# Input loads reordered, read weights cut to a quarter, all measured differences on GpSimd

## The chip, the cores and the metric

One core of one Trainium2 chip. The metric is the device time of one launch in microseconds. Engines in profile rows: PE is TensorE (PEld its weight loads), DVE is VectorE, ACT is ScalarE, POOL is GpSimd, SP is SyncE; a q behind a name is the engine's queue of instructions that issue DMAs.

## The reference

x is 1024 tokens (2 batches of 512) of 1024 channels, read as 256 heads by C = 4. Cut to what matters:

```
r = layernorm(x)                                   # the front: per token
y_o = sum_c r[h, c] * W[h, o, c]                   # "read": o = 0..2 gives q, k, v inputs
q, k, v = norm(y_o) @ qkv_w[o]; q, k = rope(q, k, pos)
a = causal softmax attention, 16 heads of 16       # then a "write" that mixes a into r
mlp: read (2 outputs), ctx as weights, silu * up, and a second write
x = x + r
W1, W2, W3 = base + mean(|w - base|) * sign(w - base)
x = x + (silu(ln(x) @ W1.T) * (ln(x) @ W3.T)) @ W2.T     # 3584 inner channels
```

The two scalars mean(|w - base|) of w1 and w3 need every element of both before the first product with a blended weight; w2's is measured later.

## The kernel before

The program has two phases. Phase one (to about 410 us) computes the attention part for 8 tiles of 128 tokens and, beside it, measures w1 and w3. Phase two is the large feed-forward product, bound by TensorE.

Phase one is cut into nodes (stage, tile, part), each on one engine. `phase_one_order` puts them in one order by the table RANK (a node is taken when all it depends on has been taken, lowest rank first), and each engine runs its own nodes in that order, waiting on semaphores. The tables WORK, LOADED and DIFFERENCE hold the planner's costs and load times; they change nothing but the assignment of banks.

The stages: `front` (per tile: layer norm statistics on DVE, power on POOL, scaling on ACT L1790, turning on PE L1406, copy L1795, read products with a block-diagonal weight `diag` on PE L1444, statistics L2129, power L2545, scaling L1803, turning, copy, qkv products L1459, rotation on DVE L2164 to L2172, turning, copy). `diag` (DVE L2336) multiplies the read weights w_in by an eye of 32 columns; it uses only rows 32c to 32c + 31 of channel c of w_in. `fill` (scores into the PSUM area quad, twice for each group of 4 heads: S for the row maxima, T turned), `use` (DVE maxima L2182 for S, ACT exponentials L1830 for T), `turnmax` (PE L1489, DVE L2191), `weigh` and `out` (PE L1479, ACT), `row`, `back` (first write and second read), `mlp`, `finish` (second write), `norm`, `turn`, `early` (the first feed-forward products).

`measure` t (0 to 55, one weight tile of 128 x 1024 each): SP loads w and base into one of three slots (L1280, L1281), the difference is taken on DVE in one instruction (L2388) or on POOL in four pieces (L2551), ACT sums the absolute values (L1878), and the slot is free. MEASURER gives 38 of the 56 to DVE (t mod 3 is 0 or 1) and 18 to POOL. Slots 1 and 2 share memory with the mlp's ctx up to t = 29, and measures from 30 on wait for the first batch's attention. `coef` needs all 56 sums, `prep` and `upper` blend the first weight tiles; ACT's first copy into xnT_hi waits for all 56 as well.

The start: SP issues ident, cmask, pos, inv and gb, then x0, x1, w_in0, wqkv, x2, x3, w_in1, x4, x5, then both write weights, and the measure loads. PE, DVE and ACT wait for the five constants (ld_const at 80). DVE then makes unit, maskb, eyer, the angles and, after ACT's two sines, the rotation tables and eye, all ahead of its first node. ACT makes the sines and waits for the tables (rope_ok) ahead of its first node. `lull` puts filler products (bf16, `unit` times `unit`, 512 columns, L1415) ahead of some PE nodes, as many as LULLS says.

## Time and profile before

| | us |
|---|---|
| median of 3 runs | 1199.28 (1198.12 to 1204.73) |
| the profiled execution's own time | 1198.74 |
| its span | 1197.0 |
| PE busy | 1162.5 (97%) |
| DVE busy | 944.9 (79%) |
| ACT busy | 714.4 (60%) |
| POOL busy | 367.9 (31%) |

The span is that of one execution as the profiler saw it. Busy time is the union of an engine's instructions; PE's ends are modelled, so a busy PE isn't one at its peak. In the stretches PEclk is the granted share of the full TensorE clock of 2.4 GHz.

### The profile page before, as it was taken

Reading aid. Unit: us, or ns where it says so; the run is one execution under the profiler, and the core shown is the slowest. Engines: PE = TensorE matmul, PEld = TensorE weight load, DVE = VectorE, ACT = ScalarE, POOL = GpSimd, SP = SyncE. Lnnn points to the kernel's source line nnn. Section 1 sums busy time; section 2 is a strip of 40 time slices with the busy share of each in tenths; the row PEclk is TensorE's granted clock in tenths of the full one; section 3 lists DMA queues with packets and bytes.
Section 4 is the critical chain, followed back from the end, with each engine's and each line's share of the span. In section 5 each row is a group of like instructions: output and inputs, shape, how many; then the busy total and the mean of one; then the engine's idle time right before and its main releaser. Section 6 shows DMA issues by size and latency. Waiting matters only on the chain.

```text
span 1197.0 us, 17179 instructions
## 1 busy us (share of the span) xinstructions
PE 1162.5 (97%) x6218; PEld 909.0 (76%) x6218; DVE 944.9 (79%) x1279; ACT 714.4 (60%) x1017; POOL 367.9 (31%) x441
## 2 busy tenths in 40 slices
PE   6998899999999999999999999999999999999998
PEld 4765565657777787888888888888888888888887
DVE  6878899788989688777877778777885687888764
ACT  3887776867778566665666556565663433333342
POOL 2333534444543424443344424353330000000000
PEclk8999999999999999999999999999999999999999
DMA  8377796645431566687667867678756968752332
GB/s 354 135 272 284 272 342 217 233 180 189 159 104 55 194 187 223 220 271 244 198 220 231 281 189 250 193 247 265 220 184 233 358 230 288 254 201 91 104 132 97
DMA packets 99064, 257.37 MB, mean 215 GB/s; under 512 B 9362, under 2 KB 23972, under 8 KB 98468
## 3 DMA queue, kind: packets, MB, share of 16 engines
q1 hardware_dynamic: 94948, 241.59, 56.0%
q0 software_dynamic: 4032, 14.68, 6.9%
q8 instruction: 50, 0.82, 0.3%
q14 instruction: 34, 0.28, 0.1%
HBM read 214.81 MB, written 41.42 MB: 214 GB/s over the span
## 4 chain that ended last, share of the span: by engine, by line
PE 79%; DVE 12%; ACT 5%; issue 3%; DMA 1%; POOL 1%; SPq 0%; ACTq 0%; DVEq 0%
PE pair L1572 30%; PE quad L1572 12%; PE quad L1619 11%; PE pair L1619 11%; DVE negwide L2182 3%; PE pair L1553 2%; PE quad L1516 1%; PE quad L1506 1%; ACT prob L1830 1%; DVE wr_q L2235 1%; PE pair L1479 1%; DVE inner L2370 1%; ACT sgate L2001 1%; PE quad L1553 1%; PE quad L1521 1%
## 5 line engine op out<-in xcount | busy, mean ns | idle before, releaser
L2551 POOL TENSOR_TENSOR raw_w<-raw_w,raw_base 128x256 f32<-128x256 f32 x224 | 197.6, 934 | 187.1 <-DMA raw_base<-in_mean_w 187.1
L2095 ACT ACTIVATE split<-grid 128x1024 fp32r<-128x1024 f32 x98 | 104.0, 1061 | 160.8 <-PE pair L1619 147.7
L2493 DVE TENSOR_TENSOR split<-grid,split 128x1024 fp32r<-128x1024 f32 x98 | 119.7, 1224 | 61.8 <-ACT split L2095 61.6
L1619 PE MATMUL quad<-split 128*128 128x512 f32 x588 | 149.3, 389 | 0.5 <-DVE hid L2500 0.5
L1619 PE MATMUL pair<-split 128*128 128x512 f32 x588 | 149.2, 389 | 0.0
L1619 PEld LDWEIGHTS quad<-split 128*128 128x128 f32 x588 | 110.3, 188 | 23.7 <-DVE split L2493 0.9
L1619 PEld LDWEIGHTS pair<-split 128*128 128x128 f32 x588 | 110.3, 188 | 23.0
L2274 DVE TENSOR_TENSOR ring_lo<-raw_base,ring_hi 128x1024 fp32r<-128x1024 f32 x56 | 71.6, 1279 | 31.4 <-ACT ring_hi L2040 25.6
L1572 PE MATMUL pair<-t_b_hi,ring_hi 128*128 128x512 f32 x224 | 88.6, 396 | 0.4 <-ACT snap L2059 0.4
L1572 PE MATMUL pair<-t_b_lo,ring_hi 128*128 128x512 f32 x224 | 87.8, 392 | 0.0
L1572 PE MATMUL pair<-xnT_hi,ring_hi 128*128 128x512 f32 x224 | 87.5, 391 | 0.3 <-ACT xnT_lo L1921 0.3
L1572 PE MATMUL pair<-xnT_lo,ring_hi 128*128 128x512 f32 x224 | 87.2, 389 | 0.0
L1572 PE MATMUL pair<-xnT_hi,ring_lo 128*128 128x512 f32 x224 | 87.2, 389 | 0.0
L1572 PE MATMUL pair<-t_b_hi,ring_lo 128*128 128x512 f32 x224 | 87.1, 389 | 0.0
L2270 DVE SCALAR_TENSOR_TENSOR raw_w<-quad,coeff,raw_base 128x1024 f32<-128x1024 f32 x52 | 66.5, 1280 | 14.2 <-ACT quad L1889 14.0
L2274 DVE TENSOR_TENSOR ring_lo<-raw_w,ring_hi 128x1024 fp32r<-128x1024 f32 x28 | 40.0, 1427 | 44.3 <-ACT ring_hi L1898 44.3
L1889 ACT ACTIVATE quad<-raw_w 128x1024 f32<-128x1024 f32 x52 | 53.1, 1020 | 17.3 <-POOL raw_w L2551 16.8
L2613 POOL DMA_DIRECT2D late<-in_w x28 | 25.0, 891 | 123.3 <-ACT late L2071 123.1
L2182 DVE TENSOR_REDUCE negwide<-quad 128x4 f32<-128x512 f32 (+3 forms) x32 | 46.9, 1487 | 4.9 <-PE quad L1509 4.6
L1572 PEld LDWEIGHTS pair<-t_b_lo,ring_hi 128*128 128x128 f32 x224 | 42.0, 188 | 9.9
L1572 PEld LDWEIGHTS pair<-t_b_hi,ring_hi 128*128 128x128 f32 x224 | 42.1, 188 | 9.7 <-ACT snap L2059 1.2
L1572 PEld LDWEIGHTS pair<-t_b_hi,ring_lo 128*128 128x128 f32 x224 | 42.1, 188 | 9.3
(331 smaller groups left out, 2760.6 us busy)
## 6 DMA issues: line engine op xcount, KB each, us to landing
raw_w<-in_w SPq DMA_DIRECT2D x56, 512.0 KB, 5.7
raw_base<-in_mean_w SPq DMA_DIRECT2D x56, 512.0 KB, 7.0
grid<-h_blocks SPq DMA_DIRECT2D x49, 512.0 KB, 3.7
late<-in_mean_w SPq DMA_DIRECT2D x28, 512.0 KB, 7.5
late<-in_w POOLq DMA_DIRECT2D x28, 512.0 KB, 6.7
grid<-in_mean_w SPq DMA_DIRECT2D x28, 512.0 KB, 4.7
h_blocks<-work SPq DMA_DIRECT2D x42, 256.0 KB, 2.8
ctxw<-in_w SPq DMA_DIRECT2D x20, 512.0 KB, 4.1
```

The source lines that it names most:

```text
L1479: a = pe.matmul(target[32 * r:32 * r + 32, first:HQ], vaug[:, b * TPB + k, head:head + 32], probs[TURN[u] % 2][:, r, at:at + cols], start= ...
L1553: a = pe.matmul(bank[:, 0:NZ], lhs, wcat[n][:, k, :], start=k == 0, stop=k == kt - 1)
L1572: a = pe.matmul(bank, ww[:, at + k, :], xx, start=first and k == 0 and n == 0, stop=k == half - 1 and n == 2, skip_group_check=not first)
L1619: a = pe.matmul(into[t], found[:, a, t * P:(t + 1) * P], found[:, b, :], start=p == 0 and n == 0 and q < 4, stop=p == PAIRS - 1 and n == 2 ...
L1889: act.activation(spare.rearrange("p a b -> p (a b)"), w[:, :], ACT.Sign).then_inc(f_sign, 1)
L2095: act.activation(splits[n % RINGS][:, 0:2, :], operands(n), ACT.Copy).then_inc(a_hi, 1)
L2182: a = dve.tensor_reduce(found.rearrange("p r j -> p (r j)"), quad[:, :, at:at + cols], AX.X, ALU.max, negate=True)
L2270: dve.scalar_tensor_tensor(w[:, :], sign, coeff[:, k:k + 1], base[:, :], ALU.mult, ALU.add).then_inc(f_w, 1)
L2274: dve.tensor_tensor(whole_of(pair[1]), source, whole_of(pair[0]).bitcast(F32), ALU.subtract).then_inc(done, 1)
L2493: dve.tensor_tensor(found[:, 2:4, :], operands(n), found[:, 0:2, :].bitcast(F32), ALU.subtract).then_inc(a_lo, 1)
L2551: a = pool.tensor_tensor(w[:, some], w[:, some], base[:, some], ALU.subtract)
L2613: pool.dma_start(lates[n % LATES][:, :], d["w2"][n], accum_op=ALU.add).then_inc(ld_add[n % LATES], 16)
```

## The change

- SP loads x0, x1, wqkv, x2, x3, a quarter of w_in1 (four DMAs of 32 partitions, 64 KB each), x4, x5 and then the measure tiles; the write weights (wcat, bias, dut) come behind measure 2's loads.
- ACT's queue loads ident, pos, inv (new semaphore ld_first), a quarter of w_in0 (four DMAs of 96 KB), cmask and gb. PE and DVE begin with ld_first; ACT waits for cmask and gb ahead of its first node.
- Angles and sines, eye and the masks become nodes of the order (`angle`, `eye`, `mask`). Waits are added where they are used: DVE at its first rotation, ACT at the copy of tile 4 (it overwrites their memory), PE at the first score unit.
- MEASURER gives all 56 measures to POOL.
- RANK is replaced as a whole, and LULLS too (78 fillers before; of the first tiles 14, 14, 13, 1 and 3 become 14, 4, 10, 1 and 2). The costs of `angle`, `eye` and `mask` are entered, and LOADED has new times.

The diff, cut to its core (the new table RANK and the later entries of LULLS are left out):

```diff
+    "angle": [("DVE", 2.1), ("ACT", 1.9), ("DVE", 1.0)],
+    "eye": [("DVE", 0.6)],
+    "mask": [("DVE", 0.6)],
...
-MEASURER = ("DVE", "DVE", "POOL")
+MEASURER = ("POOL", "POOL", "POOL")
...
-LOADED = {("front", 0, 0): 6.0, ("front", 1, 0): 8.0, ("front", 2, 0): 19.0, ("front", 3, 0): 21.0, ("front", 4, 0): 27.0,
-          ("front", 5, 0): 29.0, ("diag", 0, 0): 14.0, ("front", 0, 13): 17.0, ("diag", 1, 0): 25.0}
+LOADED = {("angle", 0, 0): 3.6, ("front", 0, 0): 4.6, ("front", 1, 0): 5.9, ("eye", 0, 0): 3.6, ("mask", 0, 0): 6.0,
+          ("diag", 0, 0): 7.5, ("front", 0, 13): 9.6, ("front", 2, 0): 10.8, ("front", 3, 0): 12.1, ("diag", 1, 0): 12.8,
+          ("front", 4, 0): 14.1, ("front", 5, 0): 15.4, ("measure", 3, 0): 27.0}
...
         after("measure", LATER - 1, 2)
+    elif stage == "diag":
+        after("eye", 0, 0)
...
     ('front', 0, 4): (14, 0, ('front', 0, 11)),
-    ('front', 0, 6): (14, 0, ('front', 0, 11)),
-    ('front', 0, 11): (13, 0, ('front', 0, 11)),
-    ('front', 0, 13): (1, 2, ('front', 0, 13)),
-    ('front', 1, 11): (3, 0, ('front', 1, 11)),
+    ('front', 0, 6): (4, 0, ('front', 0, 11)),
+    ('front', 1, 4): (10, 0, ('front', 0, 11)),
+    ('front', 0, 11): (1, 0, ('front', 0, 11)),
+    ('front', 0, 13): (2, 2, ('front', 0, 13)),
     ('fill', 3, 0): (1, 0, ('fill', 3, 0)),
...
-            sp.dma_start(ident[:, :], d["ident"]).then_inc(ld_const, 16)
-            sp.dma_start(cmask, d["cmask"]).then_inc(ld_const, 16)
-            sp.dma_start(pos_i[:, :], d["pos"]).then_inc(ld_const, 16)
-            sp.dma_start(inv[:, :], d["inv_freq"]).then_inc(ld_const, 16)
-            sp.dma_start(gb[:, :, :, :], d["gb"]).then_inc(ld_const, 16)
-            for t in range(TPB):
+            for t in range(TPB + 2):
                 sp.dma_start(x_at(t), d["x"][t]).then_inc(ld_x[t], 16)
                 if t == 1:
-                    sp.dma_start(w_in[0], d["w_in0"]).then_inc(ld_win0, 16)
                     sp.dma_start(wqkv[:, :, :], d["wqkv"]).then_inc(ld_wqkv, 16)
-            sp.dma_start(w_in[1], d["w_in1"]).then_inc(ld_win1, 16)
-            for t in (TPB, TPB + 1):
-                sp.dma_start(x_at(t), d["x"][t]).then_inc(ld_x[t], 16)
-            for n, ld in enumerate((ld_wr0, ld_wr1)):
-                sp.dma_start(wcat[n][:, :, :], d[f"wcat{n}"]).then_inc(ld, 16)
-                sp.dma_start(bias_ab[n][:, :], d[f"bias_ab{n}"]).then_inc(ld, 16)
-                sp.dma_start(dut[n][:, :], d[f"dut{n}"]).then_inc(ld, 16)
+                elif t == 3:
+                    for c in range(C):
+                        rows = slice(32 * c, 32 * c + 32)
+                        sp.dma_start(w_in[1][rows, c, :, :], d["w_in1"][rows, c]).then_inc(ld_win1, 16)
...
+                    if t == PARTS - 1:
+                        for k, ld in enumerate((ld_wr0, ld_wr1)):
+                            sp.dma_start(wcat[k][:, :, :], d[f"wcat{k}"]).then_inc(ld, 16)
+                            sp.dma_start(bias_ab[k][:, :], d[f"bias_ab{k}"]).then_inc(ld, 16)
+                            sp.dma_start(dut[k][:, :], d[f"dut{k}"]).then_inc(ld, 16)
...
                 if u == 0:
+                    pe.wait_ge(masks, 2)
...
-            pe.wait_ge(ld_const, 80)
-            pe.wait_ge(masks, 2)
+            pe.wait_ge(ld_first, 48)
+            pe.wait_ge(masks, 1)
...
+                    if t == TPB:
+                        act.wait_ge(rope_ok, 1)
+                        act.wait_ge(masks, 2)
+                        act.wait_ge(diags, 1)
...
-            act.wait_ge(angle, 1)
-            act.activation(whole_sin, ang, ACT.Sin)
-            act.activation(half_sin, ang, ACT.Sin, scale=0.5).then_inc(sines, 1)
-            act.preload_act_table_set(LN_EXP)
+            act.dma_start(ident[:, :], d["ident"]).then_inc(ld_first, 16)
+            act.dma_start(pos_i[:, :], d["pos"]).then_inc(ld_first, 16)
+            act.dma_start(inv[:, :], d["inv_freq"]).then_inc(ld_first, 16)
+            for c in range(C):
+                rows = slice(32 * c, 32 * c + 32)
+                act.dma_start(w_in[0][rows, c, :, :], d["w_in0"][rows, c]).then_inc(ld_win0, 16)
+            act.dma_start(cmask, d["cmask"]).then_inc(ld_const, 16)
+            act.dma_start(gb[:, :, :, :], d["gb"]).then_inc(ld_const, 16)
             act.wait_ge(consts, 8)
-            act.wait_ge(ld_const, 80)
-            act.wait_ge(rope_ok, 1)
+            act.wait_ge(ld_const, 32)
             for engine, stage, t, part in order:
                 if engine != "ACT":
                     continue
-                if stage == "front":
+                if stage == "angle":
+                    act.wait_ge(angle, 1)
+                    act.activation(whole_sin, ang, ACT.Sin)
+                    act.activation(half_sin, ang, ACT.Sin, scale=0.5).then_inc(sines, 1)
+                    act.preload_act_table_set(LN_EXP)
+                elif stage == "front":
...
                     if t:
                         dve.wait_ge(fr_qt, t)
+                    else:
+                        dve.wait_ge(rope_ok, 1)
...
-            dve.wait_ge(ld_const, 80)
+            def angles(part):
+
+                if part == 0:
+                    magic = float(1.5 * 2 ** 23)
+                    chained(dve.tensor_copy(posf[:, :], pos_i[:, :]))
+                    chained(dve.tensor_tensor(ang, posf[:, :].unsqueeze(2).to_broadcast([P, TILES, HALF]),
+                                              inv[:, :].unsqueeze(1).to_broadcast([P, TILES, HALF]), ALU.mult))
+                    chained(dve.tensor_scalar(turns, ang, float(1 / (2 * np.pi)), magic, ALU.mult, ALU.add))
+                    chained(dve.tensor_scalar(turns, turns, -magic, None, ALU.add))
+                    for some in two_pi_parts():
+                        chained(dve.scalar_tensor_tensor(ang, turns, -some, ang, ALU.mult, ALU.add))
+                    dve.tensor_scalar(ang, ang, 3.1415925, -3.1415925, ALU.min, ALU.max).then_inc(angle, 1)
+                else:
+                    dve.wait_ge(consts, 8)
+                    dve.wait_ge(sines, 1)
+                    chained(dve.tensor_tensor(half_sin, half_sin, half_sin, ALU.mult))
+                    for n in range(2):
+                        dve.tensor_scalar(rcos[:, :, n, :], half_sin, -2.0, 1.0, ALU.mult, ALU.add)
+                        a = dve.tensor_scalar(rsin[:, :, n, :], whole_sin, 2.0 * n - 1.0, None, ALU.mult)
+                    a.then_inc(rope_ok, 1)
+
+            dve.wait_ge(ld_first, 48)
             dve.tensor_copy(unit[:, :], ident[:, :]).then_inc(masks, 1)
-            dve.tensor_copy(maskb[:, :], cmask).then_inc(masks, 1)
-            for n in range(2):
-                dve.tensor_scalar(eyer[:, n, :], ident[:, :], 1.0 - 2.0 * n, None, ALU.mult).then_inc(eye_ok, 1)
-            magic = float(1.5 * 2 ** 23)
-            chained(dve.tensor_copy(posf[:, :], pos_i[:, :]))
-            chained(dve.tensor_tensor(ang, posf[:, :].unsqueeze(2).to_broadcast([P, TILES, HALF]),
-                                      inv[:, :].unsqueeze(1).to_broadcast([P, TILES, HALF]), ALU.mult))
-            chained(dve.tensor_scalar(turns, ang, float(1 / (2 * np.pi)), magic, ALU.mult, ALU.add))
-            chained(dve.tensor_scalar(turns, turns, -magic, None, ALU.add))
-            for part in two_pi_parts():
-                chained(dve.scalar_tensor_tensor(ang, turns, -part, ang, ALU.mult, ALU.add))
-            dve.tensor_scalar(ang, ang, 3.1415925, -3.1415925, ALU.min, ALU.max).then_inc(angle, 1)
-            dve.wait_ge(consts, 8)
-            dve.wait_ge(sines, 1)
-            chained(dve.tensor_tensor(half_sin, half_sin, half_sin, ALU.mult))
-            for n in range(2):
-                dve.tensor_scalar(rcos[:, :, n, :], half_sin, -2.0, 1.0, ALU.mult, ALU.add)
-                a = dve.tensor_scalar(rsin[:, :, n, :], whole_sin, 2.0 * n - 1.0, None, ALU.mult)
-            a.then_inc(rope_ok, 1)
-            dve.wait_ge(rope_ok, 1)
-            chained(dve.tensor_tensor(eye[:, :], ident[:, 0:32], ident[:, 32:64], ALU.add))
-            chained(dve.tensor_tensor(eye[:, :], eye[:, :], ident[:, 64:96], ALU.add))
-            dve.tensor_tensor(eye[:, :], eye[:, :], ident[:, 96:128], ALU.add).then_inc(eyes, 1)
             for engine, stage, t, part in order:
                 if engine != "DVE":
                     continue
-                if stage == "diag":
+                if stage == "angle":
+                    angles(part)
+                elif stage == "eye":
+                    chained(dve.tensor_tensor(eye[:, :], ident[:, 0:32], ident[:, 32:64], ALU.add))
+                    chained(dve.tensor_tensor(eye[:, :], eye[:, :], ident[:, 64:96], ALU.add))
+                    dve.tensor_tensor(eye[:, :], eye[:, :], ident[:, 96:128], ALU.add).then_inc(eyes, 1)
+                elif stage == "mask":
+                    dve.wait_ge(ld_const, 32)
+                    dve.tensor_copy(maskb[:, :], cmask).then_inc(masks, 1)
+                    for n in range(2):
+                        dve.tensor_scalar(eyer[:, n, :], ident[:, :], 1.0 - 2.0 * n, None, ALU.mult).then_inc(eye_ok, 1)
+                elif stage == "diag":
                     dve.wait_ge(eyes, 1)
-                    dve.wait_ge((ld_win0, ld_win1)[t], 16)
+                    dve.wait_ge((ld_win0, ld_win1)[t], 16 * C)
                     for c in range(C):
...
```

In RANK the measures stand among other stages about where they stood: the last difference at rank 788 of 1018, before at 774 of 1013; the first at 25, before at 70.

## Rows read from the trace of the kernel before

**Rows 1.** The page's chain that ended last: shares of the span.

```profile
PE 79%; DVE 12%; ACT 5%; issue 3%; DMA 1%; POOL 1%; SPq 0%; ACTq 0%; DVEq 0%
```

**Rows 2.** Stretches: us, busy PE, PEld, DVE, ACT, POOL (instructions), PEclk, DMA share, GB/s.

```profile
45.00:320.00 275.00, 258.66 (x2178) 174.83 (x2177) 238.93 (x411) 207.52 (x374) 118.33 (x146) 1.00 0.66 241
320.00:410.00 90.00, 85.25 (x405) 64.10 (x405) 78.01 (x132) 67.02 (x95) 42.33 (x47) 1.00 0.28 101
410.00:1197.00 787.00, 782.76 (x3441) 645.06 (x3439) 597.51 (x643) 415.52 (x507) 197.15 (x228) 1.00 0.66 215
```

**Rows 3.** Timeline of the start: start us, us, engine, line, what [idle before].

```profile
0.75 0.39 SPq L1253 DMA_DIRECT2D ident<-in_ident  x1
...
2.60 0.43 SPq L1257 DMA_DIRECT2D gb<-in_gb  x1
...
4.28 0.23 DVE L2304 CAST unit<-ident 128x128 bf16<-128x128 f32 x1 [4.28 <-DMA gb<-in_gb]
...
7.01 0.26 ACT L1956 ACTIVATE big<-big 128x64 f32<-128x64 f32 x1 [4.99 <-DVE big L2316]
...
7.43 1.28 ACT L1958 ACT_TABLE_LOAD   x1
...
8.88 1.28 DVE L2111 BATCH_NORM_STATS2 stat_ln<-prob 128x6 f32<-128x512 f32 x2
...
12.40 1.24 ACT L1790 ACTIVATE hid<-prob,stat_ln 128x1024 f32<-128x1024 f32 x1 [3.69 <-DVE stat_ln L2119]
...
15.46 5.25 PE L1415 MATMUL quad<-unit 128*128 128x512 bf16 x14
...
15.70 1.02 ACT L1795 ACTIVATE xT<-pair 128x1024 f32<-128x1024 f32 x1 [2.06 <-PE pair L1406]
...
20.55 1.92 PE L1444 MATMUL pair<-diag,xT 128*128 128x96 f32 x16
```

**Rows 4.** Stretches of the start, columns as in rows 2.

```profile
14.00:16.00 2.00, 2.00 (x10) 1.66 (x9) 1.97 (x3) 0.30 (x1) 0.00 (x0) 0.50 1.04 426
20.00:21.00 1.00, 1.00 (x9) 0.74 (x7) 0.00 (x0) 0.00 (x0) 0.00 (x0) 1.00 0.99 393
```

**Rows 5.** DMA issues of the first 46 us: KB each, median us to landing.

```profile
prob<-in_x SPq DMA_DIRECT2D x3, 512.0 KB, 4.4
big<-in_w_in SPq DMA_DIRECT2D x1, 1536.0 KB, 7.7
...
ident<-in_ident SPq DMA_DIRECT2D x1, 64.0 KB, 1.8
```

**Rows 6.** Stretch 45 to 320, L2388 alone: DVE busy (instructions), PEclk, DMA.

```profile
45.00:320.00 275.00, 49.74 (x38) 1.00 0.66 241
```

**Rows 7.** Chain of waits, 45 to 320 us: first and last of ten pieces of L2388.

```profile
53.66 1.13 DVE ctxw L2388
...
278.08 1.59 DVE big L2388
```

**Rows 8.** L2551 by its tiles: ns min/median/max, first and last start; then busy, mean, idle before.

```profile
L2551 POOL TENSOR_TENSOR ctxw<-ctxw x40: 718/727/1775, 46.8 to 159.3; 128x256 f32<-128x256 f32 x40
...
L2551 POOL TENSOR_TENSOR ctxw<-ctxw 128x256 f32<-128x256 f32 x40 | 32.7, 849 | 38.7 <-DMA ctxw<-in_mean_w 38.7
L2551 POOL TENSOR_TENSOR big<-big 128x256 f32<-128x256 f32 x32 | 27.3, 886 | 35.0 <-DMA big<-in_mean_w 35.0
```

**Rows 9.** L1878 (the last sums) and L1579 on xnT_hi: columns as in rows 8.

```profile
L1878 ACT ACTIVATION_READ_ACCUMULATOR big<-big x17: 185/188/210, 168.2 to 317.7; 128x1 f32 x17
...
L1579 PE MATMUL pair<-xnT_hi,eyer x4: 397/437/477, 356.0 to 368.9; 128*128 128x512 f32 x4
```

**Rows 10.** Two DVE lines: min/median/max as in rows 8, then L2248's busy and mean.

```profile
L2248 DVE TENSOR_TENSOR hid<-hid,wr_a x16: 945/956/1484, 142.1 to 379.1; 128x768 f32<-128x768 f32 x16
L2227 DVE SCALAR_TENSOR_TENSOR wr_z<-wr_b,wr_a x16: 198/200/690, 104.6 to 367.4; 128x48 f32<-128x48 f32 x16
...
L2248 DVE TENSOR_TENSOR hid<-hid,wr_a 128x768 f32<-128x768 f32 x16 | 17.1, 1072 | 0.0
```

More of the change, by code:

```diff
@@ L235, in before @@
             after("diag", 0, 0)
+        if part == 14 and t == 0:
+            after("angle", 0, 2)
         if part == 0 and t >= TPB + 2:
@@ L243, in before @@
             after("use", t - 1, 0)
+        if t == 0:
+            after("mask", 0, 0)
         if kind == "T":
@@ L629 @@
[L629 to L631 removed]
+    ("angle", 0): (0,),
+    ("angle", 1): (1,),
+    ("angle", 2): (22,),
+    ("back", 0): (212, 232, 368, 394, 464, 482, 663, 693),
+    ("back", 1): (225, 233, 369, 395, 465, 488, 674, 695),
+    ("back", 2): (226, 237, 374, 398, 468, 489, 675, 696),
@@ new lines @@
+    ("blend", 0): (851, 1014),
+    ("blend", 1): (858, 1015),
+    ("blend", 2): (870, 1016),
+    ("blend", 3): (1007, 1017),
+    ("coef", 0): (811,),
+    ("coef", 1): (816,),
+    ("coef", 2): (817,),
+    ("ctx", 0): (410,),
+    ("diag", 0): (9, 133),
+    ("dump", 0): (714, 780, 886, 915, 958, 970, 972, 1013),
+    ("early", 0): (953, 986),
+    ("early", 1): (976, 1003),
+    ("early", 2): (984, 1004),
+    ("early", 3): (985, 1008),
+    ("eye", 0): (5,),
+    ("fill", 0): (89, 107, 113, 130, 142, 151, 163, 176, 179, 194, 209, 215, 231, 235, 247, 260, 271, 274, 286, 292, 304,
+        307, 318, 326, 338, 352, 362, 382, 397, 407, 419, 428, 442, 452, 478, 494, 508, 513, 530, 539, 555, 565, 574, 590,
+        606, 616, 632, 637),
@@ new lines @@
+    ("norm", 0): (747, 828, 850, 905),
+    ("norm", 1): (798, 883, 906, 927),
+    ("norm", 2): (824, 917, 919, 936),
+    ("norm", 3): (825, 918, 935, 937),
+    ("norm", 4): (842, 938, 951, 952),
+    ("out", 0): (150, 175, 180, 187, 255, 283, 333, 353, 393, 417, 440, 446, 529, 598, 631, 647),
+    ("prep", 0): (819, 840, 849, 1002),
+    ("raw", 0): (689, 690, 761, 866),
+    ("raw", 1): (699, 728, 823, 878),
+    ("raw", 2): (756, 830, 831, 912),
+    ("row", 0): (188, 213, 354, 371, 450, 467, 649, 670),
@@ new lines @@
+    ("row", 1): (200, 214, 355, 372, 453, 470, 655, 673),
+    ("row", 2): (206, 217, 361, 383, 455, 476, 657, 677),
+    ("row", 3): (207, 218, 367, 387, 458, 480, 658, 678),
+    ("turn", 0): (925, 943, 977, 997),
+    ("turn", 1): (926, 947, 978, 999),
+    ("turn", 2): (965, 979, 991, 1005),
+    ("turn", 3): (939, 964, 990, 1006),
+    ("turn", 4): (980, 981, 994, 1009),
+    ("turn", 5): (982, 983, 998, 1010),
+    ("turn", 6): (955, 966, 992, 1011),
+    ("turn", 7): (956, 967, 993, 1012),
```

242 lines of the change are left out of this document (98 added, 144 removed).

## The prediction

> **What bounds the kernel now.** I read the chain of waits first, then stretches of time, then the first 25 us line by line. The chain [rows 1] is 79% TensorE and 12% VectorE: 144 us of VectorE, nearly all in the first 410 us. The stretches [rows 2] say why. From 410 us on TensorE is busy 782.8 of 787 us; nothing of the change lies there except that this part starts earlier or later. From 45 to 320 us, in which attention, the backs and the first mlp blocks run, TensorE is busy 258.7 of 275 us and VectorE 238.9; GpSimd has 118.3, ScalarE 207.5. So the time can change only by what goes before 410 us, and there by two things: how late the first products start, and how often the chain goes through VectorE.
>
> At the start [rows 3] VectorE begins at 4.28 us, when the fifth DMA (gb) has landed, works through masks and angles, and reaches the first tile's statistics at 8.88. ScalarE scales the tile at 12.40, TensorE turns it from 13.70 (1.97 us in the chain), and then 14 filler products hold it until 20.55, when the first read products (L1444) start. Their other operands were there earlier: xT was copied from 15.70 in 1.02, the last diag piece was written by 16.03. The granted clock was 0.50 in 14 to 16 us and 1.00 from 20 to 21 [rows 4]: half level, 1.2 GHz, then full, 2.4 GHz, after TensorE had worked without a pause from 13.7.
>
> **The change part by part. All against the profiled execution: span 1197.0, its own time 1198.7; the median of three is 1199.3, 0.5 above.**
>
> *Start.* The chain now needs ident, positions and frequencies, 3 DMAs from ScalarE's queue. SP's rows have a pitch of 0.46 us ((2.60 - 0.75)/4 [rows 3]) and ident took 1.8 us to land [rows 5]; so they are there at 0.75 + 2 x 0.46 + 1.7 = 3.4. VectorE: unit 0.23, angles 4.83 to 6.99 = 2.2, stats and aggregate 1.6, so 7.4; GpSimd's power 0.56, shift 0.15: 8.1. ScalarE can be later: nine issues end at 0.75 + 9 x 0.46 = 4.9, and gb, the last, must land (1.7 without traffic, the 4.4 of a token tile in it [rows 5]): 6.1 to 8.8. Then come both sines (0.5) and a table load of 1.28 [rows 3], perhaps two, since the one at 0.75 now stands behind DMA issues. The scaling starts between 7.9 and 11.9; I take 9.3, against 12.40. It takes 1.24; turning 1.04 (full clock) to 1.97; the copy 1.02, beside which 4 fillers fit instead of 14. First read products at 9.3 + 1.3 + 1.6 + 1.2 = 13.4 plus a hop or two, say 14.0; diag is done by 8.1 + 4 x 0.95 = 11.9 if its quarter weights (4 x 96 KB in place of 1536 KB, which took 7.7 us [rows 5]) land by 8. Gain 20.55 - 14.0 = 6.5 us. Both ends: 9 (all prompt, warm), 3 (gb late, a second table load, the clock still at half level: L1444's 1.92 us would double). The 14 fillers ahead of tile 0 start at about 3.8 and last 14 x 0.43 = 6.0, so until the turn; that is what should carry the clock over.
>
> The token tiles and wqkv now come early, 1.9 MB of read weights are no longer loaded at all (2560 KB become 640 KB; 4.8 us at 410 GB/s, the mean of the two stretches in [rows 4]), and wcat, bias and dut wait behind measure loads 0 to 2. These hide: wcat's first user is a back after 100 us. If x2 came later than its statistics (now 16 us), tile 2 would wait; it is asked for third, so no. Issuing 9 DMAs from ScalarE costs its queue 4 us in which it had nothing to do (idle 4.99 us before its first sine [rows 3]).
>
> The Trainium skill (DMA: Bandwidth & Descriptors, Issuing engines are not separate DMA queues) says that transfers issued by different engines run on the same 16 DMA engines and interleave. By it the constants compete with x0 and x1, and the late end, 8.8, would hold: start gain 4 instead of 6.5. No run here shows two hardware queues at once.
>
> *Waits added.* ScalarE waits at tile 4 for tables and diag, TensorE at the first score unit for maskb, VectorE at its first rotation (34.2 us before) for the tables. All three are written within the first 25 us or are planned ahead of the first unit (50 us before); behind each stands the whole engine, but the awaited work is ten or more us older. Cost 0; if mask slipped past the first unit, under 1 us (0.6 us of work).
>
> *Measures.* 38 of 56 differences leave VectorE: 49.7 us of 238.9 between 45 and 320 [rows 6]. Only those on the chain count directly: 10 pieces from 53.66 to 278.08, 1.13 + 1.29 + 1.22 + 1.80 + 1.13 + 0.64 + 1.13 + 1.67 + 1.82 + 1.59 = 13.4 us [rows 7]. On GpSimd each is four pieces, of which 72 took 32.7 + 27.3 us, 0.83 each [rows 8]: 38 x 4 x 0.83 = 126 us more. It had 118 of 275 there, so 244; but measures can now begin at 20 to 25 us, not at 46.8 [rows 8], so about 244 of 300, 81%. Below: nobody waits for a measure soon. The last one ended at 317.8 [rows 9]; coefficients follow at 326, and the first xnT_hi, which needs all 56, is used at 356. So some 35 us of slack. ScalarE's sums are the same.
>
> What is paid: VectorE operations with two inputs in SBUF get longer when they meet a GpSimd piece. L2227 has a median of 0.200 and a maximum of 0.690, L2248 0.956 and 1.484 [rows 10]: one piece, 0.5 us, at most. Busy time less count times minimum gives what they lost: L2248 17.1 - 16 x 0.945 = 2.0 [rows 10], in the same way L2251 1.7, L2227 1.6, L2234 0.9, together 6.2 us for 64 of them. There are two to three times as many others of their kind (L2123, L2119, L2136, L2172, the sums and splits), so I take 17 us, an estimate. It came with some 208 GpSimd operations in 45 to 410; 152 more make it x1.7, +12 on VectorE. The chain takes its share: of VectorE's busy time before 410 (239 + 78 in [rows 2] and 30 before 45 us) 144 are in the chain, 41%: +5. From both sides: 0 (met pieces off the chain) to +12.
>
> The steps behind (a gain that the next late engine takes) against the gains off the chain (36 us of measures that delayed VectorE's queue without showing in it): I set them equal. Middle: -13.4 + 5 = -8.4. Ends: 0 and -25. The latter is TensorE's own idle time there, 16.3 us by [rows 2], plus waits hidden in matmul records, perhaps 10.
>
> Sum: 1198.7 - 6.5 - 8.4 = 1183.8; on the scale of the median, **1184.5**.
>
> The Trainium skill (Perfetto Trace Analysis, Optimizing Scalar/DVE Operations) warns that GpSimd's only read port is VectorE's second one, held exclusively, "so offloading operations between those two might not help". The rows agree that there is such a block; they don't yet say that it eats the gain. That is rival A.
>
> **The rivals.** *A, the port eats the middle.* Two-input operations on VectorE meet GpSimd at work 81% of the time instead of 43%. If every one of the 373 other VectorE operations in 45 to 320 took 0.36 us more at 0.4 more of the meetings, that is 54 us, all that was taken off. Against it: operations that read PSUM show no spread. Then only the start is left: 1199.3 - 6.5 = 1193.
>
> *B, VectorE was the whole bound.* It was busy 87% of the stretch; without 50 us the stretch shrinks until TensorE has no idle time: -25, with the start 1168. For it: nearly every unit passes L2182, L2191 and the measure between. Against: ScalarE's exponentials and TensorE's scores alternate on one PSUM area, whoever else is free.
>
> *C, slower: GpSimd becomes the bound.* Its queue is in order, and a measure whose DMA isn't there holds the power and the residual operations behind it. Already its 18 measures waited 73.7 us, 4.1 each [rows 8]. From 20 us on it needs 244 and some 4 before 45 us, 248, plus 56 waits of w; the last measure passes 350 - 6 when w is over 1.36 us, and from there each further 0.1 us costs 5.6. At w = 1.6 it comes 14 us late, and that less the start's 6.5 is 1207. Against: three slots are loaded ahead, and 5 us loads fit under two measures of 3.4.
>
> *D, the start doesn't carry.* ScalarE's issues or the cold clock leave 3 us, and fills between the fronts take it: 1198, with little from the middle.
>
> **How the numbers follow.** Forecast 0.43 (1176 to 1190), A 0.19, B 0.15, C 0.13, D 0.10. A measurement tells 0.5%, 6 us, from no change: 1193.3 and 1205.3 are the borders. Faster: 0.43 + 0.15 + half of A = 0.68; same: the other half of A, all of D, and 0.01 of C = 0.20; slower: the rest of C, 0.12. The range takes in A and D, B's near half and C's weak end, so that 0.1 is left out on either side: 1170 to 1202.
>
> **What would show it.** First L1444 at 13 to 15 us; 11 or less or 17 or more makes the start wrong. No L2388 in the chain; VectorE's busy time in the first 400 us down by 35 to 40; L2248 and L2227 with medians up. GpSimd's busy share at 80% or more from 30 to 310 us. Last ScalarE sum before 340. First xnT_hi product use at about 341 instead of 356, and from there the same 787 us to the end. If the time falls by 15 but the last sum lies where first xnT_hi copies wait for it, the mechanism is C's, only cheaper. The prediction is wrong if the stretch 45 to 320 isn't shorter though VectorE has its 35 us.

## The result: slower by half a percent, and the profile after

The changed kernel takes 1209.1 us (median of 20 executions, 1197.9 to 1222.1), the kernel before 1199.9 in the same comparison. The ratio is 1.0052, 95% interval 1.0033 to 1.0072; it leaves out the one slow execution, of 1222.1 us, and is not the quotient of the two medians, which is 1.0077. The forecast was 1184.5 with 1170 to 1202 as its range: the time moved the other way and left the range.

The 20 executions fall into two groups: 8 at 1197.9 to 1202.8 us, with a mean granted clock of 0.994 to 0.996, and 12 at 1207.9 or more, with 0.985 to 0.993. The profiled one took 1201.7 (span 1200.0), so it is of the lower group, whose mean is 1199.7; a second trace, of an execution at 1208.5, comes with the experiments.

The timeline of the start of the changed kernel (start us, us, engine, line, what, idle before and releaser):

```profile
0.74 0.41 ACTq L1965 DMA_DIRECT2D ident<-in_ident  x1
...
4.87 0.47 ACTq L1972 DMA_DIRECT2D gb<-in_gb  x1
...
9.20 0.23 DVE L2345 CAST unit<-ident 128x128 bf16<-128x128 f32 x1 [9.20 <-DMA inv<-in_inv_freq]
...
15.66 1.28 ACT L1980 ACT_TABLE_LOAD   x1 [15.66 <-DMA gb<-in_gb]
...
18.68 1.24 ACT L1796 ACTIVATE hid<-prob,stat_ln 128x1024 f32<-128x1024 f32 x1
...
19.97 1.97 PE L1411 MATMUL pair<-ident,hid 128*128 128x128 f32 x8 [4.57 <-ACT hid L1796]
...
23.44 0.80 PE L1449 MATMUL pair<-diag,xT 128*128 128x96 f32 x3
```

VectorE starts at 9.20 in place of 4.28, the scaling of tile 0 at 18.68 in place of 12.40, the read products at 23.44 in place of 20.55 [rows 3]. Two waits for DMAs made that: VectorE's first for inv and ScalarE's first for gb. The DMA issues of the first 46 us (KB each, median us from issue to landing) say how long they took:

```profile
prob<-in_x SPq DMA_DIRECT2D x3, 512.0 KB, 5.1
...
pos_i<-in_pos ACTq DMA_DIRECT2D x1, 4.0 KB, 5.3
inv<-in_inv_freq ACTq DMA_DIRECT2D x1, 4.0 KB, 7.5
gb<-in_gb ACTq DMA_DIRECT2D x1, 10.0 KB, 10.7
```

On ScalarE's queue, beside SyncE's token tiles, 4 KB took 7.5 us and 10 KB 10.7; the 512 KB of a token tile took 5.1.

TensorE's clock was part of the loss. Its 14 fillers ended at 15.40, it stood idle for the 4.57 us ahead of the turn, and its granted clock was at half level, 1.2 GHz, from 18.4 to 25.2, so that the turn took 1.97 us (columns as in [rows 2]):

```profile
18.40:25.20 6.80, 5.23 (x21) 4.22 (x22) 1.01 (x4) 2.52 (x3) 0.55 (x1) 0.50 1.05 421
```

Stretches of the changed kernel, columns as in [rows 2]; the last is the one piece of the attention stage at half clock:

```profile
45.00:320.00 275.00, 259.11 (x2190) 175.91 (x2190) 210.43 (x384) 214.22 (x384) 215.65 (x289) 0.99 0.67 241
320.00:410.00 90.00, 86.12 (x411) 64.33 (x410) 80.16 (x136) 66.27 (x95) 42.67 (x47) 1.00 0.29 102
410.00:1200.00 790.00, 785.47 (x3448) 646.13 (x3446) 597.92 (x643) 415.10 (x507) 199.46 (x231) 1.00 0.66 215
...
141.20:144.70 3.50, 3.50 (x33) 1.37 (x33) 1.43 (x3) 2.92 (x5) 3.50 (x6) 0.51 0.47 192
```

VectorE did lose 28.5 us between 45 and 320, and GpSimd is busy 78% of it (81% forecast). TensorE's busy time there hardly moved: 258.7 before, 259.1 now.

A ruler for the attention stage is the row of its 24 exponentials, from the start of the first to the start of the last. It is the same work in the same sequence in every kernel here. I call the time between the two the stage. Before, then changed (ns min/median/max, first and last start in us):

```profile
L1830 ACT ACTIVATE prob<-quad x24: 1429/1453/1883, 59.8 to 259.8; 128x1536 f32<-128x1536 f32 x16, 128x2048 f32<-128x2048 f32 x8
```

```profile
L1840 ACT ACTIVATE prob<-quad x24: 1433/1452/1880, 64.5 to 264.0; 128x1536 f32<-128x1536 f32 x16, 128x2048 f32<-128x2048 f32 x8
```

The first comes 4.7 us late, and the stage takes 199.5 us against 200.0. So in this execution the late start is the whole loss, and with 38 measures taken off VectorE the stage is 0.5 us shorter.

The measures on GpSimd waited little, so rival C's condition (waits of 1.36 us a measure) was not met: three tiles together 24.3 us between 45 and 320, against 73.7 for two tiles before [rows 8].

```profile
L2580 POOL TENSOR_TENSOR ctxw<-ctxw 128x256 f32<-128x256 f32 x76 | 56.9, 779 | 12.2 <-DMA ctxw<-in_mean_w 12.2
L2580 POOL TENSOR_TENSOR part<-part 128x256 f32<-128x256 f32 x72 | 54.4, 787 | 5.7 <-DMA part<-in_mean_w 5.7
L2580 POOL TENSOR_TENSOR big<-big 128x256 f32<-128x256 f32 x68 | 53.0, 811 | 6.4 <-DMA big<-in_mean_w 6.4
```

### The profile page after: what moved, and what is told of

Same layout as the page of the kernel before. It is cut to its first block and busy times, and to the rows that moved or that the text cites. A ratio compares the mean times of both kernels' runs of the same rounds, so it can differ in the third digit from the quotient of the medians.

```text
span 1200.0 us, 17268 instructions
## 1 busy us (share of the span) xinstructions
PE 1160.0 (97%) x6200; PEld 907.3 (76%) x6200; DVE 913.7 (76%) x1241; ACT 716.7 (60%) x1019; POOL 472.6 (39%) x593
## 5 line engine op out<-in xcount | busy, mean ns | idle before, releaser
L2580 POOL TENSOR_TENSOR ctxw<-ctxw 128x256 f32<-128x256 f32 x80 | 60.2, 783 | 12.2 <-DMA ctxw<-in_mean_w 12.2
L2580 POOL TENSOR_TENSOR part<-part 128x256 f32<-128x256 f32 x76 | 57.2, 784 | 5.7 <-DMA part<-in_mean_w 5.7
L2580 POOL TENSOR_TENSOR big<-big 128x256 f32<-128x256 f32 x68 | 53.0, 811 | 6.4 <-DMA big<-in_mean_w 6.4
```

Source lines behind the costliest of these rows:

```text
L2580: a = pool.tensor_tensor(w[:, some], w[:, some], base[:, some], ALU.subtract)
```

## Experiments on the start: which load is waited for

Times are medians, with the range. The kernel before was run beside each and lay at 1199.1 to 1200.0. One execution each of e1 and e13 took 2957 and 2334 us, for a reason that nothing here shows; ranges and ratios leave them out. Several kernels here have two groups of times, as the changed kernel does, and then the median depends on how many executions fell into the upper one; the table behind e9 has the lower groups alone.

**e1: constants back on SyncE, ahead of the tokens.** The same move for pos, inv, cmask and gb; the quarter weights stay on ScalarE's queue.

```diff
+            sp.dma_start(ident[:, :], d["ident"]).then_inc(ld_first, 16)
...
             for t in range(TPB + 2):
...
-            act.dma_start(ident[:, :], d["ident"]).then_inc(ld_first, 16)
...
```

> The changed kernel, but ident, positions, frequencies, the causal mask and gb are issued by SyncE ahead of the token tiles, as before; the quarter read weights stay on ScalarE's queue. Theory S (the start is lost because the small constants on ScalarE's queue share the DMA engines with SyncE's big loads: they landed at 9.2 us, gb at 15.7, against 4.3 before): the first angles begin by 4.5 us, gb is there by 6, the first L1449 read products come at 14 to 17 us in place of 23.1, and the time falls by 5 to 9 us against the changed kernel, to about 1200 (1196 to 1203; ratio to the kernel before 0.997 to 1.002). Rival M (the measures on GpSimd cost what is lost, the start doesn't matter): the start is early but the time stays within 2 us of the changed kernel's 1209 median, ratio 1.004 or more. Rival K (the granted clock falls in the attention stage because of the new order): as M, and the mean granted clock stays at 0.987 to 0.993 in most executions.

Measured: 1192.5 us (1188.7 to 1201.3), ratio 0.995, 0.9928 to 0.9971. That is 17 us better than the changed kernel, twice what theory S said. Between the lower groups alone it is 8.4, within theory S's 5 to 9; the rest is a second effect (next section), which this kernel has in 2 executions of 11 only. Its timeline:

```profile
4.51 0.23 DVE L2345 CAST unit<-ident 128x128 bf16<-128x128 f32 x1 [4.51 <-DMA inv<-in_inv_freq]
...
9.91 1.24 ACT L1801 ACTIVATE hid<-prob,stat_ln 128x1024 f32<-128x1024 f32 x1
...
13.47 2.00 PE L1454 MATMUL pair<-diag,xT 128*128 128x96 f32 x16 [0.30 <-ACT xT L1806]
```

The forecast had the scaling at 9.3 and the products at 14.0. The working of the start was right within 0.6 us for these loads, though the three constants came 1.1 us later than the 3.4 of the forecast; it was wrong for the queue that the change gave them. The half clock at the start is gone too: this trace has none ahead of 277.9 us.

**e4: SyncE's first token tile waits for the three constants.**

```diff
+            sp.wait_ge(ld_first, 48)
             for t in range(TPB + 2):
```

> The changed kernel, with one wait: SyncE issues its first token tile only when ident, positions and frequencies have landed; they have the DMA engines to themselves. Theory S: they land 1.7 to 2.5 us after their issue, by 3.5 us, and the angles begin there instead of at 9.2; the token tiles come some 2.5 us later than now and gb still late, near 15; the scaling of tile 0 starts between 13 and 16.5 (18.7 now), the time falls by 2 to 5 us, ratio 1.000 to 1.003. Rival Q (ScalarE's queue itself is slow to start, by a fixed time, whatever else is loaded): the three land at 7.5 to 9 us again and the time is 2 to 3 us above the changed kernel's. Rival M: no change of the time though they land early.

Measured: 1198.5 (1195.9 to 1210.1), ratio 1.0009, 0.9987 to 1.0032. With nothing else in flight, ScalarE's queue is prompt; gb, which goes out among the tokens, still takes 7.5 us and gates the sines:

```profile
inv<-in_inv_freq ACTq DMA_DIRECT2D x1, 4.0 KB, 1.8
gb<-in_gb ACTq DMA_DIRECT2D x1, 10.0 KB, 7.5
```

```profile
12.08 1.28 ACT L1981 ACT_TABLE_LOAD   x1 [12.08 <-DMA gb<-in_gb]
```

So rival Q falls: the same queue takes 1.8 us for 4 KB without the token loads and 7.5 with them. The Trainium skill (DMA: Bandwidth & Descriptors, Queues, rings and completion order) says that a transfer's completion is counted on a DMA engine only after every earlier write of that engine, whichever queue it came from. The 7.5 us fit it; no run here separates that from the sharing of the engines.

**e8 and e9: which of the two waits counts.** e8 puts only the three small constants ahead of the tokens on SyncE; gb stays last on ScalarE's queue. e9 leaves all loads and moves one wait:

```diff
-            act.wait_ge(ld_const, 32)
             for engine, stage, t, part in order:
...
                     act.preload_act_table_set(LN_EXP)
+                    act.wait_ge(ld_const, 32)
```

> The changed kernel, but only ident, positions and frequencies go ahead of the tokens on SyncE's queue; mask and gb stay behind the quarter weights on ScalarE's. Theory S: VectorE and the filler products begin at 3.5 to 4.5 us, but ScalarE waits for gb, which lands near 15, ahead of its sines: the scaling of tile 0 comes at 18 to 19 as in the changed kernel, nothing is gained in the end: 1207 to 1211, ratio 1.004 or more; TensorE has a longer pause ahead of the turn. Rival (the three small ones are what the start waited for): scaling by 12, time 1193 to 1197.

> The changed kernel, but ScalarE waits for gb and the mask behind the sines and the table load instead of ahead of its whole order. All loads stay where the change put them. The constants land at 9.2 us as before and gb at 15.7. Since the wait is only moved behind the table load, the scaling of tile 0 still waits for gb: table loads and sines (4.3 us) now lie ahead of 15.7 and the scaling starts at 15.8 in place of 18.7. Theory S (each us of the start is a us of the end, and gb's landing is what gates it): first L1449 at 20 to 21, time 1203 to 1207 against the changed kernel's 1209. Rival (the small three at 9.2 are the gate, not gb): the scaling does not move by more than 0.5 us.

Measured: e8 1194.6 (1193.0 to 1219.2), ratio 0.9976, 0.9951 to 1.0001; e9 1197.7 (1192.8 to 1208.5), ratio 1.0002, 0.9976 to 1.0028. Both medians missed on the good side. In e8 gb was issued 1.8 us earlier, behind three DMAs less, and landed after 7.5 us in place of 10.7, at 10.67 and not near 15; why it took 3.2 us less is open. The scaling starts at 13.68, the read products at 18.26. The time lies in the rival's range, but by another way: the scaling still waited for gb, whose landing had moved. In e9 gb lands about where it did, but two table loads and the sines (3.0 us, and not the 4.3 of the expectation) are done by then:

```profile
15.53 1.24 ACT L1796 ACTIVATE hid<-prob,stat_ln 128x1024 f32<-128x1024 f32 x1 [1.28 <-DMA gb<-in_gb]
...
19.03 2.02 PE L1449 MATMUL pair<-diag,xT 128*128 128x96 f32 x16 [0.25 <-ACT xT L1801]
```

The scaling moved by 3.2 us, the products by 4.4: gb was the gate, and its price was the sines and table loads queued behind its wait in ScalarE's order.

The lower groups alone, against the start of the first read products in each kernel's trace (those of e8 and e9 are of upper-group executions):

| | read products, us | lower group's mean, us | executions in it |
|---|---|---|---|
| changed | 23.44 | 1199.7 | 8 of 20 |
| e4 | 19.86 | 1197.3 | 8 of 12 |
| e9 | 19.03 | 1195.6 | 7 of 12 |
| e8 | 18.26 | 1194.1 | 7 of 12 |
| e1 | 13.47 | 1191.3 | 9 of 11 |

Against the changed kernel, a microsecond of the start is 0.7 to 1.1 us of the end. By this measure e4 (2.4 us) and e9 (4.1 us) gained what theory S said. Their medians fell by 10.6 and 11.4 us because fewer of their executions are of the upper group, 4 and 5 of 12 against 13 of 21; whether that is chance, no run tells.

## Experiments on the second group: an operation of VectorE that is held

**e12: the changed kernel once more, for a second trace.** No edit.

> The changed kernel once more, for a second trace of it. Theory H: if this execution lies at 1207 or more, it shows a VectorE operation between 45 and 410 us held for 3 us or more beside an uninterrupted stretch of GpSimd pieces, with a pause of TensorE and half-level clock records right behind it; if it lies at 1203 or less, none over 2 us. Rival K: a slow execution shows half-level records without such a hold.

Measured: 1208.5 us, of the upper group. The timeline of its GpSimd, VectorE and TensorE at 193 to 206 us:

```profile
192.73 2.79 POOL L2580 TENSOR_TENSOR part<-part 128x256 f32<-128x256 f32 x4
...
195.47 0.74 POOL L2570 TENSOR_TENSOR hid<-hid,wr_s 128x256 f32<-128x256 f32 x1
...
195.86 6.63 DVE L2268 TENSOR_TENSOR hid<-hid,wr_a 128x768 f32<-128x768 f32 x1
...
196.15 5.53 POOL L2580 TENSOR_TENSOR big<-big 128x256 f32<-128x256 f32 x8
...
201.72 4.12 POOL L2580 TENSOR_TENSOR part<-part 128x256 f32<-128x256 f32 x4
...
205.78 0.38 PE L1563 MATMUL pair<-ident,wr_b 128*8 128x128 f32 x1 [5.02 <-DVE wr_b L2242]
```

L2268 takes 0.94 to 1.49 us elsewhere in this trace. Here it stands 6.63 us beside GpSimd pieces that follow each other without a pause, and it ends 0.8 us after the first pause (201.68 to 201.72). Its queue stands behind it, so TensorE waits 5.0 us for wr_b from 200.8 on, and 2.3 us into that wait its clock falls to half level for 13.7 us. Here are the window of 206 to 217 and the exponentials (columns as above):

```profile
206.00:217.00 11.00, 11.00 (x43) 7.41 (x43) 8.13 (x17) 6.72 (x12) 2.77 (x4) 0.51 0.32 112
```

```profile
L1840 ACT ACTIVATE prob<-quad x24: 1432/1452/1879, 62.6 to 270.0; 128x1536 f32<-128x1536 f32 x16, 128x2048 f32<-128x2048 f32 x8
```

207.4 us for the stage. The traces of e9 and e8 were of upper-group executions too (1205.7 and 1204.8), and show the same thing at the same operation, the fourth L2268; there too it ends 0.8 us after the first two GpSimd pieces whose rows don't overlap, with 0.10 us between them in e9 and 0.01 in e8. In order, the rows of L2268 in e9 and e8:

```profile
L2268 DVE TENSOR_TENSOR hid<-hid,wr_a x16: 943/1024/6631, 141.2 to 389.3; 128x768 f32<-128x768 f32 x16
```

```profile
L2268 DVE TENSOR_TENSOR hid<-hid,wr_a x16: 940/1066/6501, 139.2 to 388.4; 128x768 f32<-128x768 f32 x16
```

The three traces of lower-group executions (the first of the changed kernel, e1, e4) have no operation held for more than 2 us. In the first trace of the changed kernel L2268's maximum is 1493 ns, and a 0.17 us operation (L2154) took 2.04 at 135.7, until GpSimd paused; the fall of the clock at 141 stands behind that one.

**e6 and e13: the changed kernel with pauses in GpSimd's queue.** e13 has one at the end of each measure, as below; e6 counts and waits in the same way after each of the four pieces.

```diff
             def measure(t):
                 w, base = measured(t)
                 subtract(w, base).then_inc(me_pool, 1)
+                pool.wait_ge(me_pool, measured_by("POOL", t))
```

> The changed kernel, with the same gap after each measure piece on GpSimd. Theory H: the executions near 1210 (11 of 20) are those in which a VectorE operation was held, so with gaps nearly all executions lie at 1197 to 1203 and the median is 1200 (1198 to 1203), ratio 0.999 to 1.003; the start is unchanged (first L1449 at 23). Rival W: GpSimd, busy 216 of 275 us, gets 15 us more and the time grows, 1211 to 1220. Rival K: the same two groups of times as without the gaps, median 1207 to 1211.

> The changed kernel with one gap at the end of each measure on GpSimd; the start as the change has it. Theory H: the group near 1210 goes, since that group is one hold of 5.7 us and the clock's fall behind it; all executions lie at 1198 to 1203, median 1200.5, ratio 0.999 to 1.003, and L2268 is under 1.6 us everywhere. Rival R (the group is more than the hold: late constants or thin TensorE work make it too): the median stays above 1205, with half-level records of over 7 us in most executions.

Measured: e6 1204.0 (1201.3 to 1204.8), ratio 1.0031, 1.0019 to 1.0043; e13 1198.8 (1196.3 to 1201.2), ratio 0.9989, 0.9979 to 0.9998. The upper group is gone in both (three of e6's five executions lie 2.7 us above the other two, but the trace of one of the three has no hold). e6's median is just above what theory H gave: against e13 the many pauses cost 5 us. e13 has the start of the changed kernel (products at 23.32), and its rows of the exponentials and of L2268 are

```profile
L1840 ACT ACTIVATE prob<-quad x24: 1428/1452/1878, 64.1 to 260.2; 128x1536 f32<-128x1536 f32 x16, 128x2048 f32<-128x2048 f32 x8
```

```profile
L2268 DVE TENSOR_TENSOR hid<-hid,wr_a x16: 941/1146/1537, 144.0 to 381.3; 128x768 f32<-128x768 f32 x16
```

196.1 us against e12's 207.4: 11.3, of which 5.7 are the hold itself; the other 5.6 I put down to the clock, which no run takes by itself. Rival R falls. The pauses that do this are short: in e13 0.08 us behind 28 of the 56 measures; behind the others GpSimd paused for longer, as it does without the added wait.

**e7 and e10: the same two edits on e1.**

> The kernel with the constants on SyncE's queue ahead of the tokens (1192.5 median), with the same gap after each measure piece. Theory H: its few executions at 1201 (2 of 11) go, median 1190 to 1193, ratio 0.992 to 0.995, spread under 5 us. Rival W: 1195 to 1205.

> The kernel with the constants on SyncE ahead of the tokens, and GpSimd waits once at the end of each measure until its last piece has ended, in place of after every piece. Theory H (holds of VectorE last as long as GpSimd's pieces follow without a pause; the gaps after every piece took them away but cost 3 us): no VectorE operation before 410 us over 4 us longer than its minimum, at a quarter of the cost, median 1189 to 1193, ratio 0.991 to 0.994, against 1192.5 without and 1195.7 with all gaps. Rival C (the gaps' cost was the order of GpSimd's work getting later, not the gaps themselves): as with all gaps, 1194 to 1197.

Measured: e7 1195.7 (1193.9 to 1197.3), ratio 0.9968, 0.9956 to 0.998; e10 **1191.4** (1189.4 to 1194.7), ratio 0.9935, 0.9921 to 0.9949. The best of all, and without e1's executions at 1201. e7 lies above theory H's range and in rival W's; e10, with one pause per measure in place of four, is 4.3 us faster and within its own expectation, which puts the loss on the number of pauses.

Over the kernels with the new order, all measures on GpSimd and no pauses, 29 of 68 executions were of an upper group (changed kernel 13 of 21, e4 4 of 12, e8 5 of 12, e9 5 of 12, e1 2 of 11); with pauses (e6, e7, e10, e13) 0 of 27. I count as an upper group what lies 3.7 us or more above the rest of its kernel's executions.

## Experiments on the measures and the order

**e2 and e5: the kernel before, all measures on GpSimd; e5 also pauses after each piece.**

```diff
-MEASURER = ("DVE", "DVE", "POOL")
+MEASURER = ("POOL", "POOL", "POOL")
```

> The kernel before, with all 56 measured differences on GpSimd and nothing else changed (its order is the old one). Theory S: this is the good part of the change, worth the 2 to 8 us of VectorE's pieces in the chain; the time is 1191 to 1197, ratio 0.993 to 0.998. Rival M: GpSimd's in-order queue and the shared port take it back or more; the time is 1200 to 1206, ratio 1.000 to 1.005, two-input VectorE operations 12 us or more longer in sum between 45 and 410 us.

> The kernel before with all measures on GpSimd, and GpSimd waits after each piece of a measure until that piece has ended, so that its queue never runs measure pieces back to back. Theory H (VectorE is held: twice an operation of it lasted for a whole uninterrupted stretch of GpSimd pieces, 9.54 us in place of 0.94 at 223.3 and 4.55 in place of 0.17 at 158.6, and the clock fell after it): no VectorE operation before 410 us is over 1.2 us longer than its minimum any more, fewer half-level records between 45 and 410 us (3 stretches, 20 us, without the gaps), and the time falls from 1212 to 1196 to 1203, ratio 0.998 to 1.003, though each of the 224 pieces gets some 0.1 us longer. Rival W (it is GpSimd's in-order queue: power and residual operations wait behind measures): the gaps make each measure longer, so the time stays or grows, 1212 or more, ratio 1.011 or more. Rival K (the clock falls from thinner TensorE work, whatever VectorE does): time and half-level records stay within 3 us and one record.

Measured: e2 1212.1 (1209.9 to 1217.6), ratio 1.0111, 1.0092 to 1.0131, above what either theory gave; e5 1222.9 (1221.6 to 1223.9), ratio 1.0194, 1.018 to 1.0207. e2 has the longest hold of all, and is at half clock behind it:

```profile
223.28 9.54 DVE L2248 TENSOR_TENSOR hid<-hid,wr_a 128x768 f32<-128x768 f32 x1
```

```profile
232.00:243.00 11.00, 6.32 (x36) 4.65 (x37) 7.94 (x10) 6.96 (x11) 0.94 (x2) 0.53 0.27 95
```

But e5 has no hold at all and is slower still: theory H was wrong here, and rival W right. The chain of waits of e5 between 158 and 172 us, by line:

```profile
by line: POOL ctxw L2558 36.5%; POOL part L2558 29.9%; POOL hid L2527 15.0%; issue 11.9%; PE pair L1531 6.5%; ACT oT L1840 2.0%; ACT part L1878 1.5%; POOLq L2524 0.1%; POOLq L2604 0.1%; POOLq L2538 0.1%
```

In the old order ScalarE's sum of a measure stands where a VectorE difference of 1.2 us would have been done; GpSimd's 3 to 4 us are not, and ScalarE's copy oT and TensorE wait behind that sum. This is rival C's mechanism, an engine's queue in order, though no late DMA starts it here. That the new order is what avoids it I conclude from e13, which has it, all measures on GpSimd and no such loss; no run changes the order alone. TensorE's clock also fell in e5, for 24 us in four stretches, behind pauses of 1.9 to 4.7 us. So the clock follows TensorE's pauses, whoever makes them; a hold is one maker.

**e3: the changed kernel, its order as planned, but two of three measures executed on VectorE.**

```diff
         order, banks_of, had, turned_had, set_of, set_had, had_last = phase_one_order()
+        MEASURER = ("DVE", "DVE", "POOL")
+        order = [((measurer(t),) + key[1:] if key[1] == "measure" and key[3] == 1 else key) for key in order for t in key[2:3]]
```

> The changed kernel with its new start and its new order, but the measured differences shared out as before (two of three to VectorE). Theory S: the start's loss of 5 us stands and VectorE's relief is gone, so the time is worse than the changed kernel's by 2 to 8 us: 1211 to 1217, ratio 1.010 to 1.015. Rival M: it gets better than the changed kernel, 1200 to 1206. Rival K: the time goes with the clock; the mean granted clock stays at 0.987 to 0.993.

Measured: 1229.5 (1225.2 to 1238.9), ratio 1.0252, 1.0222 to 1.0282; the 24 exponentials take 223.3 us. Worse than theory S said by 12. Each order suits only its own measurer, so e2 and e3 don't price the measures alone.

**e11 and e14: the kernel before with a smaller start.** e11 has 4 fillers in place of 14 at one place; e14 also loads the read weights in quarters, on SyncE.

```diff
-    ('front', 0, 6): (14, 0, ('front', 0, 11)),
+    ('front', 0, 6): (4, 0, ('front', 0, 11)),
```

> The kernel before, with 4 filler products in place of 14 between the turn of tile 0 and its first read products, and nothing else. Theory F (10 fillers by themselves held the read products, whose operands were ready at 16.7 us): L1444 starts at 16.7 to 17.3 in place of 20.55, and the time falls by 2 to 4 us, ratio 0.997 to 0.998. Rival K (they kept the clock up): the start is at half clock until 24 or later, the products take twice as long and the time is 1199 to 1202.

> The kernel before with its order, its measures (two of three on VectorE) and its constants on SyncE, but the read weights in quarters, all on SyncE, and 4 fillers in place of 14 ahead of the first read products (these alone gave 2.5 us). Theory G (the start alone makes most of what e1 gains; the measures and the new order are worth the rest, 3 to 4 us by the shift between 60 and 260 us): L1444 at 15.5 to 17, 1194 to 1197, ratio 0.995 to 0.998. Rival (the start is all of it): 1190 to 1193. Rival (the first read products wait for angles and sines of the old order, so smaller loads bring nothing): as with fewer fillers alone, 1196.5 or more.

Measured: e11 1196.5 (1193.9 to 1197.2), ratio 0.9974, 0.9963 to 0.9984; e14 1196.3 (1194.7 to 1199.3), ratio 0.9969, 0.9959 to 0.998. One number gave 2.5 us; the quarters added nothing that can be told apart. The products start at 17.22 and 16.80. The clock came back no later for want of the ten fillers: at 19.2 us in e11, 19.6 before. The rest of e1's 7 us must lie in the new order and the measures, which no run here takes apart.

## Why the prediction was wrong, step by step

The forecast said faster and the kernel got slower: one term of its sum had the wrong sign, one was too large, and one cost was missing. Corrected by what the runs show, the sum is 1184.5 + 2.3 + 5.0 + 7.4 + 10.3 = 1209.5, against 1209.1. Only the first part of it is a test: 1184.5 + 2.3 + 5.0 = 1191.8 against e10's 1191.4. The 7.4 and the 10.3 are differences of medians, e13 less e10 and the changed kernel less e13, and lead from e10 to 1209.1 by the way they are made.

- **Start, -6.5: failed, 7.4 us by the queue and 2.3 by the carry.** The first read products are at 22.4 to 23.4 (e12 and the first trace), beyond the 17 that I had named as proof against it. The step that failed is "they are there at 0.75 + 2 x 0.46 + 1.7 = 3.4": the three constants were there at 9.2 and gb at 15.66, outside my late end of 8.8 for gb. I took ident's 1.8 us [rows 5] from a queue with nothing ahead of it. The same queue beside the token loads takes 4.4 to 10.7 us. "That is what should carry the clock over" failed with it: the fillers ended 4.6 us ahead of the turn. I had weighed the Trainium skill's sentence (DMA: Bandwidth & Descriptors, Issuing engines are not separate DMA queues), and e4 agrees with it (1.8 us for 4 KB in place of 7.5 once the tokens wait); my price for it, 2.5 us, was a third of what it took. Price: e13 1198.8 less e10 1191.4 = 7.4. With the loads right, the products start 6.2 to 7.1 us earlier (e10 14.36, e1 13.47), but the first exponential only 4.2 in e10 (55.6 for 59.8): 2.3 less than forecast. What took it on the way is open.
- **Middle, -8.4: right in sign, 5.0 too much.** e10's exponentials take 196.6 us, e13's 196.1, before 200.0: 3.4 to 3.9. e10, the exponentials and the stretch:

```profile
L1845 ACT ACTIVATE prob<-quad x24: 1427/1452/1879, 55.6 to 252.2; 128x1536 f32<-128x1536 f32 x16, 128x2048 f32<-128x2048 f32 x8
...
45.00:320.00 275.00, 261.41 (x2184) 176.82 (x2184) 209.23 (x383) 214.75 (x378) 220.98 (x292) 0.99 0.66 236
```

"I set them equal" is, as far as is known, the part that failed. VectorE's pieces went from the chain, but TensorE between 45 and 320 us is busy 258.7 before and 261.4 in e10, in 275: the next limit behind a dropped piece is TensorE's own work. TensorE's idle time there (16.3 us) shrank by 2.7, near the measured gain, and I had used it only as the far end. VectorE's busy time in the first 400 us fell by 32.9, and not by 35 to 40. The count of 208 GpSimd operations was that of the first 400 us; [rows 2] give 193 for 45 to 410, which makes the +12 a 13 and adds under 1 us to the sum.

- **Rival A: right in kind, wrong in form; 10.3 us.** I spread the port's price over every VectorE operation, half a us at most each. It came as one hold of 5.7 us, in more than half of the executions, with the clock's fall behind it: the sum had no term for either. Price: 1209.1 less e13's 1198.8. This is large because the median lies in the upper group; between the means of all executions, 1206.9 and 1198.7, it is 8.2. The Trainium skill (Perfetto Trace Analysis, Optimizing Scalar/DVE Operations) says that the two engines share a read port of SBUF, which a VectorE operation that uses two ports locks for itself. The six holds, 1.9 to 8.6 us beyond the operation's own time, in the traces of the changed kernel, e2, e8, e9 and e12 would fit such a lock, held by GpSimd's side; no run here shows that it is the port that they waited for. "One piece, 0.5 us, at most", read from a maximum of 1.484 [rows 10], was no bound: GpSimd's uninterrupted stretches became longer, up to 18.6 us in the first trace of the changed kernel (11.4 before).
- **Waits added, 0:** right; in no trace is tile 4, the first score unit or the first rotation late by them.
- **GpSimd's load and rival C:** right that it is not the bound in the new order: 78% busy, and the last sum is at 316.3 (317.7 before [rows 9]), no later. C's mechanism is what the old order shows (e2, e5).
- **Rival B:** falls. VectorE lost 28.5 us and the stage shrank by 4 at best (e13).
- **Rival D** named the mechanism of the start, with ends that were too mild: its worst start was still 3 us early, and the measured one is 2.9 late.

## What to carry to other kernels

A few KB issued on a second queue are not free of the first: whatever gates the first work should be issued ahead of the big loads, and a wait for a late load should stand behind the work that doesn't need it. When work moves from VectorE to GpSimd, look at the longest VectorE operation and not at the median, and give GpSimd's queue a wait on its own last result now and then. When TensorE is busy 94% of a stretch, its idle time there bounds what other engines' relief can gain.

## What the runs showed that I had not expected

- A VectorE operation can be held for as long as GpSimd runs without a pause: 0.94 us became 9.54, 6.63 and 6.50, and 0.17 became 4.55 (e2, at 158.6, L2136) and 2.04. Most operations beside the same stretches were not held: in the first trace of the changed kernel the fourth L2268 took 1.16 in an 18.6 us stretch of 25 pieces. What decides it is open. With a pause of 0.08 us per measure or per piece none of four traces (e6, e7, e10, e13) has a hold. But neither have those of e1 and e4, without pauses, so that the count of executions, 0 of 27 against 29 of 68, is what shows it. Whether a rarer pause would do wasn't tried.
- In the falls I followed up, TensorE's clock went to half level 1 to 5 us after the beginning of a pause, of 0.7 us (e2, at 103) to 6.6 us (e2, at 230), yet other pauses of 1 to 1.7 us passed without (before: 112, 265, 377 and 395 us).
